# A gather that opens a group of four waits for three landed rows of the group before (first graph's pass, one Trainium2 core)

## The reference, cut to what matters

```python
Q, K, V = (h @ Wq), (h @ Wk), (h @ Wv)            # each (6250, 8, 32)
score = einsum('ehd,ehd->eh', K[src], Q[dst]) / sqrt(32) + edge_bias
m     = segment_max(score, dst)
ex    = exp(score - m[dst])
attn  = ex / segment_sum(ex, dst)[dst]
out   = segment_sum(attn[:, :, None] * V[src], dst)
```

## Time and profile before

| | us |
|---|---|
| median of 3 runs | 5458.75 (5449.24 to 5463.45) |
| profiled execution, its own time | 5467.72 |
| its span | 5465.8 |
| first graph's pass, first gather to the last turn's L475 | 238.5 to 1870.7 |
| busy over the whole span: PE / DVE / ACT / POOL | 3936.6 / 3067.4 / 1863.3 / 2451.9 |

### The profile page before, as it was taken

The page is one execution under the profiler, slowest core; times in us unless marked ns, Lnnn a source line. Parts: engine busy times, 40 slices in busy tenths (PEclk is TensorE's granted clock), DMA queues, the critical chain, the costliest instruction groups (busy, mean ns, idle before and its releaser), DMA issues. The chain is left out here.

```text
span 5465.8 us, 69110 instructions
## 1 busy us (share of the span) xinstructions
PE 3936.6 (72%) x16154; PEld 2869.7 (53%) x16282; DVE 3067.4 (56%) x7623; ACT 1863.3 (34%) x5073; POOL 2451.9 (45%) x2442
## 2 busy tenths in 40 slices
PE   6867777767777659966953666666666328999999
PEld 4545545555555448866732444444444226777776
DVE  3277778877778775662063666666667773111111
ACT  1333333333333313311222444444445322333332
POOL 2256566666556360000166666666663321333332
PEclk8978888888888879987986767777777559999999
DMA  2545555555555332221173333333332360111111
GB/s 83 185 135 147 142 148 148 147 149 148 142 147 144 89 109 86 94 64 38 44 254 91 93 92 94 94 92 90 91 94 57 113 204 18 33 31 31 31 32 27
DMA packets 316126, 553.64 MB, mean 101 GB/s; under 512 B 63430, under 2 KB 213782, under 8 KB 315856
## 3 DMA queue, kind: packets, MB, share of 16 engines
q0 software_dynamic: 137120, 388.63, 26.6%
q1 hardware_dynamic: 178736, 161.98, 9.6%
HBM read 459.75 MB, written 90.62 MB: 101 GB/s over the span
## 5 line engine op out<-in xcount | busy, mean ns | idle before, releaser
L427 POOL DMA_INDIRECT attend_ring<-kv_rows,all_step_src x880 | 855.5, 972 | 669.8 <-PE attend_ps_agg L468 415.6
L927 POOL DMA_INDIRECT edge_ring<-head_rows,all_step_src x880 | 871.5, 990 | 485.9 <-issue 213.5
L963 PE MATMUL edge_ps_agg<-edge_msg,edge_sel 128*128 128x264 f32 x1760 | 670.7, 520 | 168.8 <-issue 67.9
L468 PE MATMUL attend_ps_agg<-attend_msg,attend_sel 128*128 128x264 f32 x1760 | 620.0, 456 | 179.3 <-DVE graph_qa L781 127.5
L963 PEld LDWEIGHTS edge_ps_agg<-edge_msg,edge_sel 128*128 128x128 f32 x1760 | 420.3, 259 | 292.6 <-issue 161.4
L452 PE MATMUL attend_ps_q<-graph_qa,attend_sel_t 128*128 x1760 | 538.9, 436 | 29.1 <-ACT attend_sel_t L577 23.2
L1256 DVE TENSOR_TENSOR graph_acc<-graph_acc,edge_ps_agg 128x264 f32 x880 | 369.5, 420 | 338.8 <-PE edge_ps_agg L963 166.2
L2811 DVE TENSOR_TENSOR moe_gl<-moe_ps_h,moe_act 128x341 f32<-128x341 f32 x210 | 107.9, 514 | 776.8 <-PE moe_ps_h L2729 776.8
L781 DVE SCALAR_TENSOR_TENSOR graph_qa<-graph_qa,all_step_same,attend_ps_agg 128x264 f32 x880 | 421.6, 479 | 190.8 <-remote 138.3
L468 PEld LDWEIGHTS attend_ps_agg<-attend_msg,attend_sel 128*128 128x128 f32 x1760 | 333.6, 213 | 350.9 <-issue 155.6
L2729 PE MATMUL moe_ps_h<-experts_w,moe_xt 128*128 x1680 | 501.8, 451 | 0.6 <-ACT moe_xt L2760 0.6
(11 more groups left out here) (424 smaller groups left out, 6404.4 us busy)
## 6 DMA issues: line engine op xcount, KB each, us to landing
attend_ring<-kv_rows,all_step_src POOLq DMA_INDIRECT x880
edge_ring<-head_rows,all_step_src POOLq DMA_INDIRECT x880
kv_rows<-qkv_kv SPq DMA_DIRECT2D x25, 512.0 KB, 3.0
experts_w<-in_w_t SPq DMA_DIRECT2D x16, 682.0 KB
attend_mask<-run_starts SPq DMA_DIRECT2D x440, 8.1 KB
edge_mask<-run_starts SPq DMA_DIRECT2D x440, 8.1 KB
head_rows<-hds_hh SPq DMA_DIRECT2D x25, 264.0 KB
qkv_x<-in_x SPq DMA_DIRECT2D x25, 256.0 KB, 3.2
```

The lines of the kernel that those rows point to most:

```text
L427: nc.gpsimd.indirect_dma_start(ring[:, step % RING1, :], None, g.kv_rows, bass.IndirectOffsetOnAxis(g.step_src[:, step:step + 1], 0)).then ...
L468: nc.tensor.matmul(ps_agg[i % SUM_BANKS][:, 0:AGG], sel[:, q % 2, u % QU, :], msg[:, q % 2, u % QU, :], start=True, stop=True).then_inc(s_ ...
L927: nc.gpsimd.indirect_dma_start(ring[:, n % slots, u, :], None, g.head_rows, bass.IndirectOffsetOnAxis(g.step_src[:, step:step + 1], 0)).th ...
L963: nc.tensor.matmul(ps_agg[i % BANKS][:, 0:AGG], sel[:, q % 2, u % QU, :], msg[:, q % 2, u % QU, :], start=True, stop=True).then_inc(s_agg, 1)
```

## The change

Three things are changed, all in `attend_edges`:

- The fourth gather of a group counts on a semaphore of its own (`landed_last`, 11 more semaphores). `landed` now counts the first three.
- Who read `landed` for all four rows now waits for both: POOL's messages, and DVE's products (the first two steps of a group wait for `landed`, the other two for `landed_last`).
- From the 45th gather on, one that opens a group waits in addition until the first three rows of the group before have landed. The gather of place 8, ahead of which POOL's messages stand, does not.

```diff
-        landed = m.sems_of_pool("row", groups)
+        landed, landed_last = m.sems_of_pool("row", groups), m.sems_of_pool("last_row", groups)
...
                 k = b * quarters + quarters - 1
-                pool.wait_ge(landed[k % groups], (k // groups + 1) * (16 * QU))
+                pool.wait_ge(landed[k % groups], (k // groups + 1) * (16 * (QU - 1)))
+                pool.wait_ge(landed_last[k % groups], (k // groups + 1) * 16)
...
                 if step >= RING1:
                     pool.wait_ge(s_agg, step - RING1 + 1)
+                    if step % QU == 0 and (step - RING1) % CH != CH // 2:
+                        group = step // QU - 1
+                        pool.wait_ge(landed[group % groups], (group // groups + 1) * (16 * (QU - 1)))
+                to = landed_last if step % QU == QU - 1 else landed
                 nc.gpsimd.indirect_dma_start(ring[:, step % RING1, :], None, g.kv_rows,
                                              bass.IndirectOffsetOnAxis(g.step_src[:, step:step + 1], 0)
-                                             ).then_inc(landed[step // QU % groups], 16)
+                                             ).then_inc(to[step // QU % groups], 16)
...
                 if pair % 2 == 0:
-                    v.wait_ge(landed[group % groups], (group // groups + 1) * (16 * QU))
+                    v.wait_ge(landed[group % groups], (group // groups + 1) * (16 * (QU - 1)))
                     if k >= 1:
                         v.wait_ge(s_red, group)
+                else:
+                    v.wait_ge(landed_last[group % groups], (group // groups + 1) * 16)
```

## The result

| us | before | changed |
|---|---|---|
| median of four runs each, same chip | 5456.1 (5449.24 to 5463.45) | 5421.82 (5408.26 to 5424.41) |
| profiled execution / its span | 5467.72 / 5465.8 | 5422.54 / 5420.8 |
| the pass, first to last turn's L475 (L480 now) | 287.0 to 1870.7: 1583.7 | 289.5 to 1817.2: 1527.7 |
| a turn (54 of them) | 29.33 | 28.29 |

The ratio is 0.9933 (0.9910 to 0.9956): 34 us faster, where 145 were forecast. The pass is 56 us shorter in the two profiled executions; what follows it took 8 us more.

The account below looks back on a forecast made before the run. Everything in a turn was taken as in series, DVE nearest to a bound, with PE's completions late during long gather runs. Gains 124 + 21 + 0 = 145 us, from 5467.72 to 5323, median 9 lower: 5314 us; range 5222 to 5430.

Parts of the forecast that it names:

- end wait: DVE's wait at the turn's last add (L781) for PE's late sum, 134.5 us in 48 waits, 2.8 us each.
- the term of 124: Gain at DVE's last add of a turn: 134.5 us less 0.21 us 48 times; bounds 0 and 134.5.
- The scan's 43.0 us: DVE's "remote" wait at the scan L696, 27 waits; half, 21 us, taken as gain, bounds 0 and 43.0.
- rival A: Four gathers in a row are already too many; 1.3 to 2.0 us of each end wait stay; 5399; chance 0.2.
- B: The change doesn't do it: late sums come from something else in full turns; 5459, within 10; chance 0.11.
- (1): POOL's wait at place 12, inside the run of eight gathers: the gather starts 0.9 us later, splitting the run into fours.
- (2): POOL's waits at places 0 and 4: nothing is lost at place 0, and place 4 costs nothing.
- (3): POOL's gathers and messages behind the waits: 0.9 us is covered; all three waits biting make 24.8 us a turn.
- Rival C: POOL's waits see landings late too; at 5.3 us, 31.1 us a turn, 82 us more: 5541; chance 0.07.
- The clock: PE's granted clock, 0.87 in the common turn, might rise with shorter stalls; bounds 0 and 143 us, taken as 0.
- The rule that spoke against it: Issue a DMA early, wait late; the change does the opposite, so nothing is gained and time stays at 5459.

## Why the prediction was right and wrong

**Right: what waits, and what releases it.** "A long unbroken run of gathers holds PE's completions back" and, on the first chip, runs of four hold back almost none: 2.1 us are left of the end wait's 134.5, so the term of 124 was there to be had. The scan's 43.0 us went whole, and L713 (L706) did not take it over, 9.8 against 50.2 us; I had counted half. Of rival A, which had about 100 us left, nearly nothing was seen; B is refuted. (Against B the prediction has waits "ten times as long" in rows 12; 10.30 and 7.95 us are three to four times the end wait's 2.8.)

**Wrong: the pause.** The step that failed is (1) with (2) and (3): "the gather starts ... 0.9 us later", "nothing is lost" at place 0, place 4 "costs nothing", and "with all three waits biting ... 24.8 us a turn, below any turn forecast here". The wait's end took 3.2 + 0.16 us there, from an ordinary load of 256 KB issued by SP. Measured is 4.4 to 4.5 us from the third gather's start, so 2.0 us for each wait and not 0.9. Of the 1.1 us between them some 0.5 are the landing (3.7 and not 3.2) and 0.6 are POOL's start after it (0.76 and not 0.16; the 0.16 stood behind POOL's own messages, where no landing was awaited). The second part decided: with 3.7 us and the old 0.16 the sum would have been 26.2 us, still below the forecast turn. As measured it is 16 x 1.25 + 2.13 + 3 x 2.0 = 28.1 us, against 28.29 a turn. (The 2.13 should have been 1.85, since one interval of 1.25 is already in it; that makes 27.9.) That is above the turn of 26.7 that I forecast, and POOL, not DVE or PE, sets it. The error of 1.1 us for a wait is 3.3 us a turn, of which the slack of 1.9 us (26.7 less 24.8) takes a part. Of the 111 us that are missing, 89 are the pass (145 forecast, 56 won), 8.5 lie behind it and 2.5 ahead of it; the last 11 are the profiled executions, of which the one before lies 11.6 us over its median and the changed one 0.7.

That place 4 "costs nothing" is refuted by itself: with the waits at 0 and 12 alone the turn is 26.5 us, with place 4 too 28.4. Step (3) also covered the wait with "half a turn" between a gather and its product. That is cover for one late gather, and none for an engine whose every turn is longer than the others': a delay on POOL that comes back each turn adds up until it is the bound.

**Rival C** had the right mechanism and the wrong reason. Its formula, 22.1 us and three intervals less 2.3 each, gives with the measured 4.47 us 22.1 + 3 x 2.17 = 28.6. It was to come about by landings held back like PE's completions; in fact 4.4 to 4.5 us is what they take on both kinds of chip. Its threshold, 4.8 us, wasn't reached, so it stayed below before's 29.3, by 0.3 us of landing time. The Trainium skill, "DMA: Bandwidth & Descriptors", section "Anatomy of one DMA — SWDGE (gpsimd) path", fits 2.0 us and the bytes over 436 GB/s, some 2.6 us for these 256 KB by my estimate. The 3.7 us of landing measured here are further from it than from SP's load.

**The clock**, put at nothing, did rise a little: 0.87 to 0.90 granted in the pass, where PE's busy time fell from 1134.6 to 1099.5 us. PE is not the bound of the new turn, so no run shows what that was worth.

**The rule that spoke against it**, issue early and wait late, from the Trainium skill, "DMA: Bandwidth & Descriptors", section "Rules for kernel authors", would have had no gain at all. On chips with completions on time it is borne out, with 3.1% lost; on those with late ones the gain is 0.7%.

**What I couldn't know from one trace** is that its bound is not the kernel's alone. No engine waits by "remote" for the sums in any profile of the chips on which before takes 5012 to 5021 us, in eight of the ten groups of runs; there the forecast's whole gain doesn't exist. (Three of these profiles have 72 to 81 us of "remote" at ACT's L582 alone, and in them too only 148 of the 220 rows of L445 are recorded.)

**No version run beats before everywhere.** The one that loses least on time and still gains with late completions is, by the last table, the wait at place 12 alone: within 0.3% of before on time (1.0009, 1.0012, 0.9997, 0.9997), and with late completions a turn of 28.3 us against 28.6 for the change and 29.7 without. Over some 52 turns that would make about 16 us less than the change there, some 5405 us; places 0 and 12, at 27.6, some 5370, and 0.9% lost on time. Both are estimates from a few turns in one kernel. Neither ran whole on such a chip.

## What to carry to other kernels

Take the price of a wait from the same kind of transfer, queue and size; where there is none, carry the largest one that would still leave the forecast standing (here 3.9 us: 24.8 and the slack of 1.9, over three waits), and ask whether it can be excluded. Count the waiting engine's own start after the landing as a term too. Add up the whole period of every engine that gets a recurring wait, slack or not: work ahead covers a delay once. And see the bottleneck on a second chip before building on a wait that the profile can't name.

## What the runs showed of the hardware

- The same kernel takes 5012 to 5021 us on some chips and 5456 to 5466 on others (medians), 9% more, with all executions of a group within 0.5%. The profiles of the first kind have no "remote" wait for a sum. In the others these stand at the sums of both graph passes (135.2 us in the second one's add L1256 as well) and behind long runs of gathers. The granted clock of the kernel before, over the whole, is 0.86 to 0.87 on the first kind and 0.84 on the other. The one chip met twice was on time both times, and none was met in both conditions; whether it goes with the chip or with something else at the time, and what it is, is not known.
- On a chip of the second kind, during a run of eight gathers 1.25 us apart, DVE sees a matmul's completion 1.6 to 4.2 us late (the sums of step 15 in 51 of 52 turns). With runs of four and 2.2 us of idle time between them nine of 880 sums are late by more than 1 us, at most 1.7. Pauses only 0.6 us longer than none, at places 0 and 12, leave a third of the wait by "remote" (49.6 of 134.5 us).
- A gather of 128 rows of 2 KB, issued by POOL, is seen by a wait on POOL some 4.3 to 4.8 us after it began (medians), on both kinds of chip, with other gathers in flight. On the first kind that is 3.7 us of landing and 0.76 us until POOL's next gather starts; the second kind's traces lack too many semaphore updates to split it. It was about the same for the second, third and fourth row of a group.
